# Adding the second expert buffer onto the output inside the DMA engines

## The chip, the cores and the metric

One core of a Trainium2 chip runs the whole kernel. The metric is device time in microseconds (us) from the first to the last instruction with what lies around it, as a median of three runs. A profiled execution of the same program gives a trace, and its span is the time from the first to the last instruction that it shows.

## The reference, cut to what matters

The reference builds 8 sequences of 768 tokens of 256 numbers (256 image tokens from a state-space kernel, 512 text tokens), applies one attention layer with a residual, and then a mixture of eight experts with a residual. Only the last step matters here:

```python
logits = xf @ Wr + br
topk_w, topk_idx = jax.lax.top_k(logits, TOP_K)        # TOP_K = 2 of 8 experts for each token
gate = ...                                             # softmax of the two, zero for the others
h = jax.nn.relu(jnp.einsum('th,ehf->etf', xf, W1) + b1[:, None, :])
y = jnp.einsum('etf,efh->eth', h, W2) + b2[:, None, :]
out = jnp.einsum('te,eth->th', gate, y)
h = h + out                                            # the residual, 6144 tokens x 256 float32 = 6.29 MB
```

## The kernel before, in words

The program is a row of five blocks (`with nc.Block()`), each with a stream of instructions for every engine. No engine enters a block before all have left the one before; on leaving, each executes a DRAIN, and GpSimd gathers the others and releases them. The trace puts these instructions down to the line of the `with`: L118 (`vandermonde`), L508 (`attention`), L906 (`route`), L1241 (`experts`) and L1428 (the last block, in `program`).

`vandermonde` also has GpSimd write zeros from SBUF over the DRAM buffer `acc2_d`, as eight DMAs of 768 KB in rows of 6 KB (L158). `route` computes the residual `h1` and stores it in the DRAM buffer `acc_d` (one DMA of 768 KB for each sequence, on ScalarE's queue), picks two experts for each token, and scatters the normalised tokens into `xs_d`, sorted by expert (96 indirect DMAs of 128 rows each, L960). Each expert's list is filled up with padding rows; a padding row carries a row number from TOK = 6144 on, which is why both accumulators have P = 128 rows more than there are tokens.

`experts` goes through 104 tiles of 128 rows. For each, SyncE loads the rows and the expert's weights W1, TensorE turns the rows and does both products, ScalarE does the relu, VectorE adds the bias and scales by the gate, and GpSimd adds the 128 results of 1 KB each to rows of DRAM by an indirect DMA with `compute_op=ALU.add` (L1340). Even tiles go to `acc_d`, odd tiles to `acc2_d`, so that the two DMAs in flight never meet in a row; the one for tile j waits until that of tile j - 2 has landed (`added[q]`). At the end GpSimd waits for the last of both.

The last block adds the two buffers: SyncE loads `acc_d` (L1432) and ScalarE's queue loads `acc2_d` (L1441) into SBUF, sequence by sequence, VectorE adds them (L1448), and SyncE stores each sum into `out` (L1435). SyncE's last wait is for the eight stores.

In the trace both DRAM buffers appear under the one name `acc_d`, and every DMA that GpSimd issues is on the queue q0, called software_dynamic; q1 is SyncE's and q10 ScalarE's.

Of the kernel before, what the change touches and what calls it, by code (L numbers as in the profile page):

```python
# [17 lines left out]
P = 128  # L18
NB, SEQ, D = 8, 768, 256
# [4 lines left out]
TT = SEQ // P  # L24
IT = IMG // P
KC = D // P
TOK = NB * SEQ
# [10 lines left out]
F32 = mybir.dt.float32  # L38
# [3 lines left out]
ALU = mybir.AluOpType  # L42
# [4 lines left out]
def hold(eng, sem, value):  # L47

    eng.wait_ge(sem, value)
    eng.nop(nofuse=True)  # L50
# [1146 lines left out]
def experts(nc, sem, io, ident, xs_d, acc_d, acc2_d, exp_i, src_i, held_by, weights):  # L1197
# [5 lines left out]
    with ExitStack() as ctx:  # L1203
        def sb(name, shape, dt=F32):
            return ctx.enter_context(nc.sbuf_tensor(name, shape, dt))
# [5 lines left out]
        hT, y = sb("e_hT", [P, 2, FF]), sb("e_y", [P, RING, D])  # L1211
# [6 lines left out]
        added = [sem(f"e_added{q}") for q in range(2)]  # L1218
# [6 lines left out]
        def loop(eng, tile):  # L1225

            for n in range(RING):
                tile(n, n)
            with eng.Fori(1, NT // RING - 1) as k:
                for n in range(RING):  # L1230
                    tile(k * RING + n, n)
            for n in range(RING):
                tile(NT - RING + n, n)
# [7 lines left out]
        with nc.Block() as block:  # L1241
            @block.sync
            def _(sp):
                def load(j, n):
                    row = sp.value_load(at(src_i, j), min_val=0, max_val=SLOTS - P)
                    sp.dma_start(x[:, n, :], xs_d[bass.ds(row, P), :]).then_inc(x_in[n], 16)

                def load_w1(j, n):
                    ex = sp.value_load(at(exp_i, j), min_val=0, max_val=NE - 1)
                    sp.dma_start(w1[:, n], io["W1"][bass.ds(ex, 1)].rearrange("o (c p) f -> p (o c) f", p=P)).then_inc(w1_in[n], 16)  # L1250

                for n in range(RING):
                    load(n, n)
                    load_w1(n, n)

                def tile(j, n):
                    if more(j, RING):
                        hold(sp, xt_done, j + 1)
                        hold(sp, gate_ready, j + 1)
                        load(j + RING, n)  # L1260
                        hold(sp, h_done, j + 1)
                        load_w1(j + RING, n)

                loop(sp, tile)
# [68 lines left out]
            @block.gpsimd  # L1333
            def _(pool):
                def tile(j, n):
                    hold(pool, y_ready, j + 1)
                    q = n % 2
                    if not (isinstance(j, int) and j < 2):
                        hold(pool, added[q], (j >> 1) * 16)
                    pool.indirect_dma_start(out=(acc_d, acc2_d)[q], out_offset=bass.IndirectOffsetOnAxis(ap=row_i[:, n:n + 1], axis=0),  # L1340
                                            in_=y[:, n, :], in_offset=None, compute_op=ALU.add).then_inc(added[q], 16)

                loop(pool, tile)
                for q in range(2):
                    pool.wait_ge(added[q], NT // 2 * 16)
# [38 lines left out]
def program(nc, x, txt, log_dt, inv_A_real, A_imag, B_ri, Wq, Wk, Wv, Wo, Wr, br, W1, b1, W2, b2, rotary, out):  # L1384
    io = dict(x=x, txt=txt, log_dt=log_dt, inv_A_real=inv_A_real, A_imag=A_imag, B_ri=B_ri, Wo=Wo, Wr=Wr, br=br,
              W1=W1, b1=b1, W2=W2, b2=b2, rotary=rotary, Wq=Wq, Wk=Wk, Wv=Wv)
    img_d = nc.dram_tensor("img_d", (NB, IMG, D), F32, kind="Internal").ap()
    oT_d = nc.dram_tensor("oT_d", (NIT, P, 2, SEQ), F32, kind="Internal").ap()
    acc_d = nc.dram_tensor("acc_d", (TOK + P, D), F32, kind="Internal").ap()
    acc2_d = nc.dram_tensor("acc2_d", (TOK + P, D), F32, kind="Internal").ap()  # L1390
    xs_d = nc.dram_tensor("xs_d", (SLOTS, DX), F32, kind="Internal").ap()
    with ExitStack() as ctx:
        def sb(name, shape, dt=F32):
            return ctx.enter_context(nc.sbuf_tensor(name, shape, dt))

        def sem(name):
            return ctx.enter_context(nc.semaphore(name))

        ident = sb("ident", [P, P])
        wr, br = sb("wr", [P, KC, NE]), sb("br", [P, NE])  # L1400
        with ExitStack() as held:
            def early(name, shape):
                return held.enter_context(nc.sbuf_tensor(name, shape, F32))

            wq, wk, wv = early("wq", [P, KC, 2, HEADS * DH // 2]), early("wk", [P, KC, 2, KV * DH // 2]), early("wv", [P, KC, KV * DH])
            loaded = sem("loaded")
            vandermonde(nc, sem, io, ident, img_d, acc2_d, wq, wk, wv, wr, br, loaded)
            attention(nc, sem, io, ident, img_d, oT_d, wq, wk, wv, loaded)
        wo = sb("wo", [P, KV * 2, D])
        h1 = sb("h1", [P, NB, TT, D])  # L1410
        run, base = sb("run", [P, NE]), sb("base", [P, NE])
        exp_i, src_i = sb("exp_i", [P, NT], I32), sb("src_i", [P, NT], I32)
        tail_i, held_by = sb("tail_i", [P, NE], I32), sb("held_by", [P, NT])
        with ExitStack() as held:
            def weight(name, shape):
                return held.enter_context(nc.sbuf_tensor(name, shape, F32))

            weights = (weight("ew2", [P, NE, FC, D]), weight("eb1", [P, NE, FC]), weight("eb2", [P, NE, D]))
            route(nc, sem, io, ident, img_d, oT_d, xs_d, acc_d, h1, run, base, exp_i, src_i, tail_i, held_by, wo, wr, br, weights, sem("weights_in"))
            experts(nc, sem, io, ident, xs_d, acc_d, acc2_d, exp_i, src_i, held_by, weights)  # L1420
        even, odd = sb("f_even", [P, NB, TT * D]), sb("f_odd", [P, NB, TT * D])
        even_in, odd_in = ([sem(f"f_{n}_in{b}") for b in range(NB)] for n in ("even", "odd"))
        summed, f_stored = sem("f_summed"), sem("f_stored")

        def rows(d, b):
            return d[SEQ * b:SEQ * b + SEQ, :].rearrange("(p t) d -> p (t d)", p=P)

        with nc.Block() as block:  # L1428
            @block.sync
            def _(sp):  # L1430
                for b in range(NB):
                    sp.dma_start(even[:, b], rows(acc_d, b)).then_inc(even_in[b], 16)  # L1432
                for b in range(NB):
                    sp.wait_ge(summed, b + 1)
                    sp.dma_start(out[b].rearrange("(p t) d -> p (t d)", p=P), even[:, b]).then_inc(f_stored, 16)  # L1435
                sp.wait_ge(f_stored, 16 * NB)

            @block.scalar
            def _(act):
                for b in range(NB):  # L1440
                    act.dma_start(odd[:, b], rows(acc2_d, b)).then_inc(odd_in[b], 16)  # L1441

            @block.vector
            def _(v):
                for b in range(NB):
                    v.wait_ge(even_in[b], 16)
                    v.wait_ge(odd_in[b], 16)  # L1447
                    v.tensor_tensor(even[:, b], even[:, b], odd[:, b], ALU.add).then_inc(summed, 1)  # L1448


def rotary_tables():
# [29 lines left out]
```

## Time and profile before

| | |
|---|---|
| median of three runs | 2363.81 us (2360.35 to 2363.94) |
| the profiled execution | 2364.61 us, span 2362.8 us |
| TensorE busy over the span | 87% |
| VectorE, ScalarE, GpSimd busy | 76%, 45%, 37% |
| the last block (start to end of the span) | 2314.8 to 2362.8 us |

Busy shares are averages over five blocks with different limits. For this change only the end of `experts` and the last block have to be read closely. Times in a view count from the span's start.

### The profile page before, as it was taken

How to read it: one execution, taken by the hardware profiler on the slowest of the kernel's cores; microseconds unless marked ns; L12 is line 12 of the kernel's file. 1: busy time of each engine (PE TensorE's matmuls, PEld its weight loads, DVE VectorE, ACT ScalarE, POOL GpSimd, SP SyncE). 2: the span in 40 equal slices, each digit the busy share in tenths (PEclk: the TensorE clock that was granted, in tenths of full speed). 3: DMA queues.
4: the chain of work that ended last, by engine and by line, in shares of the span. 5: the costliest groups of instructions: out<-in, count | busy, mean ns of one | idle time of the engine just before them, and what ended most of it. 6: DMA issues, size and time to landing. Idle time of an engine off the chain costs nothing. (4 is left out here: it accounts for less than half of the span.)

```text
span 2362.8 us, 58785 instructions
## 1 busy us (share of the span) xinstructions
PE 2066.4 (87%) x21124; PEld 1253.3 (53%) x21125; DVE 1786.8 (76%) x3243; ACT 1073.8 (45%) x2468; POOL 883.5 (37%) x841
## 2 busy tenths in 40 slices
PE   0458999999999999999999999985999469999990
PEld 0423444444444444444444444432888469999990
DVE  8549999999999999999999999991355524444442
ACT  2025655655565565556556556551111124444430
POOL 1023264264254354344444444301143524444440
PEclk9989999999999999999999999996999779999995
DMA  5133633633644544544444354335677268988878
GB/s 156 26 85 85 152 102 100 159 107 98 152 113 101 146 108 112 136 114 115 125 118 122 100 125 128 99 92 168 219 265 258 102 172 214 211 213 208 212 177 324
DMA packets 194723, 343.87 MB, mean 146 GB/s; under 512 B 48592, under 2 KB 127952, under 8 KB 194512
## 3 DMA queue, kind: packets, MB, share of 16 engines
q1 hardware_dynamic: 159952, 289.18, 44.2%
q0 software_dynamic: 20736, 32.91, 7.0%
q10 hardware_dynamic: 13824, 18.88, 2.2%
q8 instruction: 143, 2.34, 0.4%
q14 instruction: 68, 0.56, 0.1%
HBM read 228.00 MB, written 105.02 MB: 141 GB/s over the span
## 5 line engine op out<-in xcount | busy, mean ns | idle before, releaser
L706 ACT ACTIVATE a_prob<-ps_s,a_nmax 128x768 f32<-128x768 f32 x768 | 685.9, 897 | 582.0 <-DVE a_nmax L793 582.0
L793 DVE TENSOR_REDUCE a_nmax<-ps_s 128x1 f32<-128x768 f32 x768 | 695.0, 944 | 51.8 <-PE ps_s L637 46.7
L799 DVE STREAM_TRANSPOSE a_probT<-a_prob 128x768 f32<-128x768 f32 x768 | 700.3, 950 | 1.2 <-PE ps_o L644 1.2
L637 PE MATMUL ps_s<-a_kT,a_qT 64*128 64x384 f32 x3072 | 621.8, 519 | 51.3 <-ACT a_prob L706 46.8
L644 PE MATMUL ps_o<-a_probT,a_vrep 32*64 32x384 f32 x12288 | 560.9, 491 | 6.1 <-DVE a_probT L799 4.5
L637 PEld LDWEIGHTS ps_s<-a_kT,a_qT 64*128 64x128 f32 x3072 | 262.5, 188 | 391.9 <-ACT a_prob L706 275.4
L769 POOL TENSOR_TENSOR a_o<-a_o,a_invrow 128x1536 f32<-128x1536 f32 x32 | 110.0, 3438 | 791.8 <-ACT a_o L714 791.8
L644 PEld LDWEIGHTS ps_o<-a_probT,a_vrep 32*64 32x64 f32 x12288 | 243.3, 132 | 293.6 <-issue 129.6
L466 POOL TENSOR_TENSOR a_prod<-a_raw,a_table 128x384 f32<-128x384 f32 x304 | 294.3, 1001 | 28.4 <-DVE a_qp L471 21.3
L1340 POOL DMA_INDIRECT acc_d<-e_y,e_row_i x104 | 161.6, 1554 | 249.6 <-DVE e_y L1360 246.5
L1283 PE MATMUL ps_eh<-e_xT,e_w 128*128 128x128 f32 x1664 | 204.8, 277 | 0.0
L971 PE MATMUL ps_ra<-wo,r_oT 128*128 128x256 f32 x768 | 180.7, 397 | 23.1 <-DMA r_oT<-oT_d 23.1
L1290 PE MATMUL ps_ey<-ew,e_hT 128*128 x832 | 196.6, 379 | 0.0
L1283 PEld LDWEIGHTS ps_eh<-e_xT,e_w 128*128 128x128 f32 x1664 | 196.2, 194 | 0.1
L1321 ACT ACTIVATE e_hT<-ps_eh,e_b_now 128x128 f32<-128x128 f32 x416 | 118.6, 368 | 159.6 <-PE ps_eh L1283 104.0
L623 PE MATMUL ps_o<-a_xT,wq 128*128 128x384 f32 x512 | 185.8, 501 | 0.0
L971 PEld LDWEIGHTS ps_ra<-wo,r_oT 128*128 128x128 f32 x768 | 151.5, 200 | 45.6 <-issue 23.7
L1290 PEld LDWEIGHTS ps_ey<-ew,e_hT 128*128 128x128 f32 x832 | 150.2, 190 | 16.1
L960 POOL DMA_INDIRECT xs_d<-r_xn,r_idx x96 | 92.5, 963 | 168.7 <-DVE r_idx L1136 139.5
L706 ACT ACTIVATION_READ_ACCUMULATOR a_prob<-ps_s,a_nmax 128x1 f32 x768 | 151.1, 197 | 0.0
L623 PEld LDWEIGHTS ps_o<-a_xT,wq 128*128 128x128 f32 x512 | 91.0, 189 | 88.9 <-issue 25.6
L1358 DVE TENSOR_TENSOR e_y<-ps_ey,eb 128x256 f32<-128x256 f32 x104 | 44.2, 425 | 105.9 <-PE ps_ey L1290 105.9
(210 smaller groups left out, 1345.7 us busy)
## 6 DMA issues: line engine op xcount, KB each, us to landing
e_w<-in_L_ffn_W_dram SPq DMA_DIRECT2D x104, 512.0 KB, 4.2
a_qT<-q_d SPq DMA_DIRECT2D x124, 384.0 KB, 9.0
a_vrep<-v_d SPq DMA_DIRECT2D x128, 192.0 KB, 3.8
a_invrow<-inv_d SPq DMA_DIRECT2D x64, 384.0 KB, 5.2
oT_d<-a_o SPq DMA_DIRECT2D x32, 768.0 KB, 3.2
r_oT<-oT_d SPq DMA_DIRECT2D x64, 384.0 KB, 7.8
q_d<-a_qp SPq DMA_DIRECT2D x31, 768.0 KB, 3.7
e_x<-xs_d SPq DMA_DIRECT2D x104, 132.0 KB, 3.3
```

The lines of the kernel that those rows point to most:

```text
L466: eng.tensor_tensor(scratch[n], a, f, ALU.mult).then_inc(done, 1)
L623: last = pe.matmul(X[:, 0:HALF], w, xn[:, k, HALF * c:HALF * c + HALF], start=(k == 0), stop=(k == KC - 1))
L637: last = pe.matmul(S[:, s % 2, r, 0:HALF], qT[rows, par, 2 * hp + c, P * t:P * t + P], kT[rows, par, :], start=True, stop=True)
L644: last = pe.matmul(O[DH * c:DH * c + DH, q, 0:HALF], vrep[rows, j % NQ, j // NQ, :], keys(par, c, j, rows), start=(j == 0), stop=(j == NJ ...
L706: act.activation(prob[:, s % RING, :].rearrange("p (r k) -> p r k", r=2), S[:, s % 2, :, 0:HALF], ACT.Exp, bias=nmax[:, s % RING:s % RING ...
L793: v.tensor_reduce(nmax[:, s % RING:s % RING + 1], S[:, s % 2, :, 0:HALF], AX.XY, ALU.max, negate=True).then_inc(max_ready, 1)
L799: v.transpose(turned(par, s), prob[:, s % RING, :]).then_inc(t_ready, 1)
L971: last = pe.matmul(A[:, t % 3, 0:D], oT[:, q, c // 2, c % 2, P * t:P * t + P], wo[:, c, :], start=(c == 0), stop=(c == KV * 2 - 1))
L1283: last = pe.matmul(H[:, q, P * f:P * f + P], w1[:, n, c, P * f:P * f + P], xT[:, q, P * c:P * c + P], start=(c == 0), stop=(c == KC - 1))
L1290: last = pe.matmul(Y[:, q, 0:D], hT[:, q, P * c:P * c + P], w2[:, bass.ds(ex, 1), c, :], start=(c == 0), stop=(c == FC - 1))
L1321: last = act.activation(hT[:, q, P * f:P * f + P], H[:, q, P * f:P * f + P], ACT.Relu, bias=b1_now[:, n, f:f + 1], scale=1.0)
L1340: pool.indirect_dma_start(out=(acc_d, acc2_d)[q], out_offset=bass.IndirectOffsetOnAxis(ap=row_i[:, n:n + 1], axis=0), in_=y[:, n, :], in_o ...
```

## The change

The buffer `acc_d` is no longer a DRAM buffer of its own but the output tensor itself, so `route` stores the residual into `out` and the even tiles are added onto `out`. `acc2_d` loses its 128 rows beyond the tokens. The indirect DMA of a tile now has a bound: rows whose number is over TOK - 1, the padding rows, are skipped. The last block becomes eight DMAs that GpSimd issues, each of which adds one sequence of `acc2_d` onto `out`, from DRAM to DRAM, in pieces of 6144 bytes, followed by one wait for all of them.

```diff
                     pool.indirect_dma_start(out=(acc_d, acc2_d)[q], out_offset=bass.IndirectOffsetOnAxis(ap=row_i[:, n:n + 1], axis=0),
-                                            in_=y[:, n, :], in_offset=None, compute_op=ALU.add).then_inc(added[q], 16)
+                                            in_=y[:, n, :], in_offset=None, compute_op=ALU.add, bounds_check=TOK - 1, oob_is_err=False).then_inc(added[q], 16)
...
-    acc_d = nc.dram_tensor("acc_d", (TOK + P, D), F32, kind="Internal").ap()
-    acc2_d = nc.dram_tensor("acc2_d", (TOK + P, D), F32, kind="Internal").ap()
+    acc_d = out.rearrange("b s d -> (b s) d")
+    acc2_d = nc.dram_tensor("acc2_d", (TOK, D), F32, kind="Internal").ap()
...
         with nc.Block() as block:
-            @block.sync
-            def _(sp):
+            @block.gpsimd
+            def _(pool):
                 for b in range(NB):
-                    sp.dma_start(even[:, b], rows(acc_d, b)).then_inc(even_in[b], 16)
-                for b in range(NB):
-                    sp.wait_ge(summed, b + 1)
-                    sp.dma_start(out[b].rearrange("(p t) d -> p (t d)", p=P), even[:, b]).then_inc(f_stored, 16)
-                sp.wait_ge(f_stored, 16 * NB)
-
-            @block.scalar
-            def _(act):
-                for b in range(NB):
-                    act.dma_start(odd[:, b], rows(acc2_d, b)).then_inc(odd_in[b], 16)
-
-            @block.vector
-            def _(v):
-                for b in range(NB):
-                    v.wait_ge(even_in[b], 16)
-                    v.wait_ge(odd_in[b], 16)
-                    v.tensor_tensor(even[:, b], even[:, b], odd[:, b], ALU.add).then_inc(summed, 1)
+                    pool.dma_start(rows(acc_d, b), rows(acc2_d, b), accum_op=ALU.add, max_dma_last_dim=6144).then_inc(summed, 16)
+                pool.wait_ge(summed, 16 * NB)
```

## Rows read from the trace of the kernel before

**Rows 1.** Timeline of 2285 to 2363: start us, us, engine, line, what

```profile
2302.50 1.55 POOL L1340 DMA_INDIRECT acc_d<-e_y,e_row_i  x1 [1.97 <-DVE e_y L1360]
...
2304.46 1.55 POOL L1340 DMA_INDIRECT acc_d<-e_y,e_row_i  x1 [0.41 <-issue]
2314.81 4.06 SPq L1432 DMA_DIRECT2D f_even<-acc_d  x8
2314.83 4.25 ACTq L1441 DMA_DIRECT2D f_odd<-acc_d  x8
2321.78 1.76 DVE L1448 TENSOR_TENSOR f_even<-f_even,f_odd 128x1536 f32<-128x1536 f32 x1 [18.13 <-DMA f_odd<-acc_d]
2323.56 26.66 SPq L1435 DMA_DIRECT2D out_dram<-f_even  x8
...
2348.11 1.76 DVE L1448 TENSOR_TENSOR f_even<-f_even,f_odd 128x1536 f32<-128x1536 f32 x1 [1.96 <-DMA f_odd<-acc_d]
```

**Rows 2.** DMA view of 2315 to 2363: GB/s in 40 slices, queues

```profile
GB/s 41 287 420 394 435 420 425 415 416 425 410 430 415 420 415 415 415 410 420 420 410 425 420 415 425 410 410 430 415 425 420 435 420 425 425 425 435 420 297 5
DMA packets 3457, 18.88 MB, mean 393 GB/s; under 512 B 384, under 2 KB 384, under 8 KB 3456
```

**Rows 3.** Instructions of L1428 (leaving the last block), durations in ns

```profile
L1428 SPq COMPARE_BRANCH  x1: 38/38/38, 2362.5 to 2362.5; - x1
...
L1428 SPq EVENT_SEMAPHORE  x1: 17/17/17, 2362.8 to 2362.8; - x1
```

**Rows 4.** DMA view of 2304 to 2306.5: GB/s in 40 slices, packets

```profile
GB/s 0 0 0 0 0 0 0 0 0 16 131 98 33 66 115 115 131 49 33 66 115 197 213 147 180 99 131 115 49 0 0 0 0 0 0 0 0 0 0 0
DMA packets 144, 0.13 MB, mean 52 GB/s; under 512 B 16, under 2 KB 144, under 8 KB 144
```

**Rows 5.** DMA view of 2305.2 to 2305.6: packets

```profile
DMA packets 62, 0.06 MB, mean 149 GB/s; under 512 B 4, under 2 KB 62, under 8 KB 62
```

**Rows 6.** DMA view of 2304 to 2315: packets, MB, share of 16 engines

```profile
q0 software_dynamic: 288, 0.26, 21.0%
```

**Rows 7.** DMA view of 8 to 40: packets, MB, share of 16 engines

```profile
q0 software_dynamic: 1152, 6.29, 48.2%
```

**Rows 8.** Issues by GpSimd: ns min/median/max, first and last start us

```profile
L158 POOL DMA_DIRECT2D acc_d<-v_zero x8: 531/532/763, 10.2 to 14.1; - x8
...
L1340 POOL DMA_INDIRECT acc_d<-e_y,e_row_i x104: 1552/1552/1612, 1921.8 to 2304.5; - x104
...
L960 POOL DMA_INDIRECT xs_d<-r_xn,r_idx x96: 954/960/1129, 1705.2 to 1893.9; - x96
```

**Rows 9.** Waits of all engines, 1980 to 2300: total us, times, longest

```profile
POOL acc_d L1340 <- DVE e_y L1360: 184.7, 85, 2.5
```

**Rows 10.** Busy time by window: PE, PEld, DVE, ACT, POOL, PEclk, DMA share, GB/s

```profile
2090.00:2200.00 110.00, 110.00 (x765) 102.36 (x764) 45.26 (x207) 45.33 (x149) 46.57 (x30) 1.00 0.89 212
```

**Rows 11.** DRAIN of GpSimd on leaving four blocks, by line

```profile
L118 POOLq DRAIN  x1: 714/714/714, 30.2 to 30.2; - x1
...
L906 POOLq DRAIN  x1: 7914/7914/7914, 1896.6 to 1896.6; - x1
...
L1241 POOLq DRAIN  x1: 6142/6142/6142, 2308.4 to 2308.4; - x1
...
L1428 POOLq DRAIN  x1: 46/46/46, 2314.8 to 2314.8; - x1
```

More of the change, by code:

```diff
@@ L1420, in program @@
             experts(nc, sem, io, ident, xs_d, acc_d, acc2_d, exp_i, src_i, held_by, weights)
-        even, odd = sb("f_even", [P, NB, TT * D]), sb("f_odd", [P, NB, TT * D])
-        even_in, odd_in = ([sem(f"f_{n}_in{b}") for b in range(NB)] for n in ("even", "odd"))
-        summed, f_stored = sem("f_summed"), sem("f_stored")
+        summed = sem("f_summed")
         def rows(d, b):
```

## The prediction

> **What bounds the kernel now.** I read the page first and saw that TensorE's 87% is an average which says nothing about the end. So I took the timeline of the last 80 us [rows 1], where the reader is to see a part without TensorE: the last indirect add is issued at 2304.46, nothing is issued for ten microseconds, and from 2314.8 the last block runs until 2362.8, 48.0 us. The DMA view of that part [rows 2] says what bounds it: 18.88 MB pass at 410 to 435 GB/s in nearly every slice. Three times 6.29 MB go through the sixteen DMA engines: both buffers in, the sum out. VectorE's eight additions of 1.76 us [rows 1] lie inside the transfers. So the last block is bound by DMA bytes, and the change is worth what it does to those. The steady part of `experts` is bound elsewhere: TensorE is busy 110 of 110 us there [rows 10], and GpSimd waits for VectorE's result before each indirect add, 184.7 us in 85 waits, 2.17 us each [rows 9].
>
> **The change, part by part.** *The residual into `out`.* The eight stores in `route` have the same size and the same queue, only another address. Nothing.
>
> *The bound on the indirect add.* The trace has no bounded DMA. Per tile GpSimd's instruction takes 1.552 us; the plain scatter of as many rows takes 0.960 us [rows 8], so one more thing to do for each row has cost 0.59 us. I take half of that, 0.3 us, for a comparison of each row number, with nothing and 0.6 us as bounds. In the steady part it hides in the 2.17 us for which GpSimd waits anyway; only over 2.17 us per tile would GpSimd become the bound. At the end the last two issues stand close together (2302.50 and 2304.46, 0.41 us apart [rows 1]), so they are paid nearly in full: 2 x 0.3 = +0.6 us, bounds 0 and +1.2. Skipped padding rows save DMA time; there are at most 13,312 - 12,288 = 1,024 of them, and DMA isn't what the block waits for. Nothing.
>
> *The last block.* Removed are 24 DMAs over SBUF and the additions, 48.0 us from entering the block to the end of the span. Added are eight DMAs on GpSimd's queue. Their time has four terms.
>
> First the start. GpSimd's direct DMAs of the same shape take 0.76 us for the first and 0.53 us for each further one [rows 8], 4.5 us for eight; the data of the first needs some 4 us, so only the first issue is exposed. From the end of an issue (2304.46 + 1.55 = 2306.01) to the first packets I estimate 0.6 us, as the slices of the issue before show: it ends at 2304.05, and the packets begin in the tenth slice of 0.0625 us from 2304 [rows 1, 4]. Together 1.4 us.
>
> Then the data, the disputed cost: accumulating from DRAM onto DRAM in pieces of 6 KB stands nowhere in the trace. There are 1,024 pieces, 64 for each engine. Nearest are the indirect adds of 1 KB pieces from SBUF. In their best slice they move 213 GB/s [rows 4], just half of the 425 GB/s at which plain transfers run [rows 2]; that is what it takes if an engine reads both addends one after the other and writes while it reads. It gives 6.29 MB / 213 GB/s = 29.5 us, the lower bound. Over 0.4 us in the middle of the same add they average 149 GB/s [rows 5]: 42.2 us. Over whole adds, the reported packet time is 21.0% of 11 us x 16 = 37 us for 256 rows, 0.144 us per KB [rows 6], and six times that for 64 pieces gives 55.5 us, the upper bound. Plain 6 KB pieces from SBUF take 48.2% of 32 us x 16 / 1,024 = 0.241 us each, 25.5 GB/s per engine [rows 7], near full rate: in large pieces what is fixed vanishes. The averages of the small adds lie low because each add has only eight pieces per engine and begins and ends slowly; 64 pieces of 6 KB in a row don't. So I take the best slice, lowered as the long run of rows 2 (about 418) stands to its best slice (435): 29.5 / 0.96 = 31 us.
>
> A rule of the Trainium skill says the same of the mechanism ("Collectives: The Full Stack", "The bandwidth ceiling: the fold count and why AG ≠ RS ≠ AR"): a reducing transfer costs twice a copy, because it needs two source reads on one ring, not because of the addition. By it the data would take about 31 us too; the 213 against 425 GB/s agree. But a row of "DMA: Bandwidth & Descriptors", "Latency and other measured facts", gives copies between HBM tensors 207 to 214 GB/s per direction. Read as a limit on reading plus writing HBM, it would give the three accesses of this addition some 44 us; no transfer here shows a copy from DRAM to DRAM.
>
> Third the landing. Before, the last data lie in the last but one slice of rows 2 (until some 2361.8) and SyncE goes on at 2362.5 [rows 3]: 0.7 us.
>
> Last the leaving. Before, SyncE's path from there to the end is 0.3 us [rows 3]. Now GpSimd is last, and its DRAIN stands ahead of the end. It took 0.71 us in the block where GpSimd had issued eight direct DMAs of this size, but 7.9 and 6.1 us in the two blocks with indirect ones, and 0.05 us where it had issued none [rows 11]. I take the 0.7 us of the like kind, with 0 and 7.9 as bounds.
>
> The sum: 1.4 + 31 + 0.7 + 0.7 + 0.3 = 34.1 us in place of 48.0, which is -13.9; with the +0.6 of the bound -13.3. Span 2362.8 - 13.3 = 2349.5; the profiled execution lies 1.8 us above its span, so 2351.3, and 0.8 above the median, so 2350.5. I say 2351.
>
> **The rivals.** *A: three accesses to DRAM count like three transfers.* The half rate of the small adds (one read of DRAM, one write) is explained as well if a DMA engine's way to DRAM carries reads and writes together. Then an addition from DRAM has three accesses: 18.87 MB at about 420 GB/s, 44.9 us. The block is 1.4 + 44.9 + 0.7 + 0.7 + 0.3 = 48.0 us, and the kernel is at 2363.8 + 0.6 = 2364. For it speaks that the best slice is exactly half in both readings; against it, that loads and stores together never show what the DRAM itself can take. The trace can't tell it from mine.
>
> *B: the rate between.* DRAM read and written at once (three accesses at 31 us make 609 GB/s, more than any long stretch of rows 2 shows) slows the pieces to about 149 GB/s [rows 5]: 42.2 us, 45.3 for the block, 2361 to 2362. That counts as no change, since a measurement of this kernel can tell about 0.2%, 4.7 us, from no change. Between 31 and 39 us of data the kernel is still faster by more.
>
> *C, slower: the accumulating pieces don't overlap.* If an engine finishes reading, adding and writing one piece before the next, as the 0.144 us per KB of rows 6 would have it, the data take 55.5 us, the block 58.6, and the kernel is at 2363.8 + 10.6 + 0.6 = 2375. It decides from 48.0 + 4.7 - 0.6 - 3.1 = 49.0 us of data on, which is 0.128 us per KB. For it speaks that the last adds, with no other traffic beside them, have such packet times; against it the 213 GB/s slice.
>
> *D: the DRAIN takes its long form.* If it costs 6.1 us [rows 11] because of how accumulating DMAs are issued, add 5.4 us: my case goes to 2356, still faster, and A to 2369, slower.
>
> *E: the change doesn't do what it says.* If the bound skips nothing in the data but only in the sum, time is the same; that alone moves no number.
>
> **How the numbers follow.** My case has 0.5 (with D in it 0.08), the stretch between it and B that is still faster by over 0.2% another 0.07; A 0.2, of which a quarter with D; B 0.1; C with all data over 49 us 0.13. Faster thus 0.57; same 0.15 + 0.1 = 0.25; slower 0.05 + 0.13 = 0.18. The likeliest time is 2351, with 2347 to 2358 as its own range (the data at 29.5 us and no cost of bound or DRAIN gives 2363.8 - 16.1 = 2348, and a little for run to run; data at 33 us and D gives 2358). The range reaches from there over B and A: 2347 to 2369. It leaves out C, with 0.13, and some at the low end.
>
> **What would show it right or wrong.** In the trace of the changed kernel: the eight issues take about 4.5 us on GpSimd, and q0 moves 6.29 MB at about 200 GB/s, in 31 us (A: 140, C: 113). The last block begins within 1 us of 2315. GpSimd's DRAIN on leaving it is under 1 us (D: 6 or more). Indirect adds take under 2.2 us each, and the tile period in `experts`, with TensorE at 110 of 110 us, stays. The prediction is wrong if DRAM to DRAM accumulation is bound by accesses to DRAM rather than by reads through the engine, or if the bounded add takes over 3.7 us (1.55 + 2.17), when GpSimd would set the pace of all 104 tiles.

## The result, and the profile after

The changed kernel takes 2346.66 us (median of four runs, 2342.57 to 2351.24), the kernel before 2362.34 us in the runs beside them. The ratio is 0.9936, with a 95% interval from 0.9918 to 0.9955: 15 us faster. A second set on another occasion (`e9_changed_again` below) gave 0.9936 again, 0.9923 to 0.9948. I had forecast 2351. The median lies 0.3 us under the 2347 at which my range began; the ratio on the median I started from gives 0.9936 x 2363.81 = 2348.7. In time the interval of the ratio reaches from 11 to 19 us, and the 13.9 us that the trace below shows for the last block lie in it.

The profiled execution has a span of 2349.5 us, where the sum had 2349.5. That it fits to the tenth is luck: this was the longest of the four executions, the others had spans of 2340.8, 2343.8 and 2345.9 us, and two of the terms were off in opposite directions, as shown below. First the timeline of the changed kernel from 2299 to its end (start us, us, engine, line, what):

```profile
2303.16 1.55 POOL L1340 DMA_INDIRECT out_dram<-e_y,e_row_i  x1 [1.97 <-DVE e_y L1360]
...
2305.18 1.55 POOL L1340 DMA_INDIRECT acc_d<-e_y,e_row_i  x1 [0.47 <-issue]
2315.92 6.80 POOL L1430 DMA_DIRECT2D out_dram<-acc_d  x8 [9.19 <-PEq L1426]
```

Then the DMA view of its last block, 2315 to 2349 (GB/s in 40 slices of 0.85 us; packets; the software queue's packets, MB and share of the 16 engines):

```profile
GB/s 0 10 0 123 224 231 181 173 217 217 217 224 224 202 202 217 202 224 231 210 188 217 217 217 224 217 181 217 224 210 224 224 210 195 217 210 217 231 43 0
DMA packets 1153, 6.30 MB, mean 185 GB/s; under 512 B 128, under 2 KB 128, under 8 KB 1152
...
q0 software_dynamic: 1152, 6.29, 92.1%
```

And the instructions with which it leaves the last block, now L1426 (durations in ns, first and last start in us):

```profile
L1426 POOLq COMPARE_BRANCH  x1: 33/33/33, 2348.4 to 2348.4; - x1
L1426 POOLq DRAIN  x1: 696/696/696, 2348.6 to 2348.6; - x1
```

The reader is to see three things. The last block runs from 2315.4 to 2349.5, 34.1 us, where [rows 1] and [rows 3] had 48.0. Its data arrive at about 213 GB/s, the mean of the fifth to the 38th slice, half of the 420 of [rows 2]; but only 6.29 MB pass, not 18.88, so half the rate still wins. Up to the last indirect add nothing has changed but the time of day: it starts at 2305.18 in place of 2304.46 [rows 1], and the first one already started as much later (1922.5 in place of 1921.8 [rows 8]). The 0.7 us came before any changed instruction of the experts ran, and `route`, with its stores now into `out`, is as long as before: from GpSimd's DRAIN on leaving `attention` to the one on leaving `route` it is 1625.4 to 1896.8, and 1625.1 to 1896.6 before.

### The profile page after: what moved, and what is told of

It reads as the page before. It is cut to its first block and busy times, and to the rows that moved or that the text cites. A ratio compares the mean times of both kernels' runs of the same rounds, so it can differ in the third digit from the quotient of the medians.

```text
span 2349.5 us, 58857 instructions
## 1 busy us (share of the span) xinstructions
PE 2066.1 (88%) x21124; PEld 1253.1 (53%) x21125; DVE 1773.3 (75%) x3235; ACT 1075.1 (46%) x2468; POOL 889.9 (38%) x849
## 5 line engine op out<-in xcount | busy, mean ns | idle before, releaser
L769 POOL TENSOR_TENSOR a_o<-a_o,a_invrow 128x1536 f32<-128x1536 f32 x32 | 110.0, 3437 | 791.8 <-ACT a_o L714 791.8
L1340 POOL DMA_INDIRECT out_dram<-e_y,e_row_i x52 | 80.7, 1552 | 137.4 <-DVE e_y L1360 134.5
```

The costliest lines, as they stand in the source:

```text
L769: pool.tensor_tensor(flat, flat, invrow[:].rearrange("p h t q s -> p (h t q s)"), ALU.mult).then_inc(o_done, 1)
```

## The experiments

Each kernel was compared with the kernel before on the same chip. Where an expectation speaks of a span, the span of the changed kernel's profile, 2349.5, is meant.

**1. The bound alone** (`e1_bound_alone`), on the kernel before:

```diff
                     pool.indirect_dma_start(out=(acc_d, acc2_d)[q], out_offset=bass.IndirectOffsetOnAxis(ap=row_i[:, n:n + 1], axis=0),
-                                            in_=y[:, n, :], in_offset=None, compute_op=ALU.add).then_inc(added[q], 16)
+                                            in_=y[:, n, :], in_offset=None, compute_op=ALU.add, bounds_check=TOK - 1, oob_is_err=False).then_inc(added[q], 16)
```

> The kernel before with nothing changed but the bound on the indirect add (its last block stays as it was). My theory, that the bound costs nothing that shows and the gain is all in the last block: ratio to before 1.000, within 0.2%; the instruction 1.55 us, and at most 0.1 us lost per issue at the end. Rival, that skipping rows is itself part of the gain of 0.64%: ratio 0.997 or less.

Measured: ratio 1.0001, 0.9992 to 1.0010. To 0.1%, some 2 us, the bound costs and brings nothing. The issue group of its trace shows why no time went missing: a MOVE of 29 ns ahead of each is new, and the instruction itself is as long as in [rows 8]:

```profile
L1340 POOLq MOVE  x104: 29/29/38, 1918.6 to 2301.4; - x104
L1340 POOL DMA_INDIRECT acc_d<-e_y,e_row_i x104: 1552/1552/1612, 1919.4 to 2302.1; - x104
```

So within these 2 us the gain is that of the last block.

**2. A plain copy in place of the addition** (`e2_copy_pool`), on the changed kernel; the addition is left out:

```diff
-                    pool.dma_start(rows(acc_d, b), rows(acc2_d, b), accum_op=ALU.add, max_dma_last_dim=6144).then_inc(summed, 16)
+                    pool.dma_start(rows(acc_d, b), rows(acc2_d, b), max_dma_last_dim=6144).then_inc(summed, 16)
```

> The changed kernel with the eight transfers of the last block as plain copies from DRAM to DRAM, so the odd tiles' buffer overwrites the output and is not added. Theory 1, an engine reads both addends one after the other and writes meanwhile: a copy has one read, a 6 KB piece takes some 240 ns in place of 479, the data take 15.5 us and the span falls by 15 us against the changed kernel, to some 2334. Rival A, reads and writes of DRAM share one way: two accesses in place of three, so 2/3 of 30.5 us if the addition was bound by it, 20 us, span 2339; or, if a DRAM to DRAM copy is as slow as the skill's figure of 207 to 214 GB/s per direction has it, 30 us and no difference at all.

Measured: ratio 0.9893, 0.9876 to 0.9910; span 2334.3 us. The DMA view from 2310 to 2335:

```profile
GB/s 0 0 0 13 216 305 403 383 403 354 285 324 305 206 275 364 344 354 265 256 364 295 246 275 206 256 374 354 462 374 324 324 334 265 344 207 20 0 0 0
...
q0 software_dynamic: 1152, 6.29, 78.1%
```

The copy is faster than the addition, but its data take about 20 us (slices 4 to 37 of 0.625 us, the two outer ones nearly empty), 310 GB/s, where theory 1 had 15.5 and rival A 20. The rate jumps between 206 and 462, unlike the even row of the addition. The size came out as A had it, and for a copy theory 1 was wrong; this run alone would speak for A. That the span is 2334.3, just as theory 1 had it, says nothing: this execution entered its last block at 2310.7 and not at 2315.4, and the block took 23.6 us, 10.5 less than the changed kernel's 34.1 and not 15 less.

**3. The same copy from SyncE** (`e6_copy_sync`, a single run):

```diff
-            @block.gpsimd
-            def _(pool):
+            @block.sync
+            def _(sp):
                 for b in range(NB):
-                    pool.dma_start(rows(acc_d, b), rows(acc2_d, b), accum_op=ALU.add, max_dma_last_dim=6144).then_inc(summed, 16)
-                pool.wait_ge(summed, 16 * NB)
+                    sp.dma_start(rows(acc_d, b), rows(acc2_d, b), max_dma_last_dim=6144).then_inc(summed, 16)
+                sp.wait_ge(summed, 16 * NB)
```

> As the plain copy from GpSimd (the odd tiles' buffer overwrites the output and is not added), but issued by SyncE. Theory 1: data 15.5 us again, since the issuing engine doesn't set the rate; the start is shorter by about 1 us, and GpSimd's DRAIN on leaving is under 0.1 us in place of 0.7. If the software queue itself were slow, this one would be clearly faster than the copy from GpSimd.

Measured: 2359.73 us, on another chip, whose runs of the kernel before have a median of 2389.36 us. What that chip takes longer lies in `route`, long before the last block: from GpSimd's DRAIN on leaving `attention` to the one on leaving `route` it is 297.6 us here and 271.4 us in the changed kernel's trace. Its DMA view from 2334 to 2358:

```profile
GB/s 0 0 0 14 236 307 369 440 358 358 348 348 266 236 297 348 287 348 317 266 277 236 287 317 113 266 348 328 430 379 399 379 297 410 317 287 215 61 10 0
...
q1 hardware_dynamic: 1152, 6.29, 82.1%
```

Again some 20 us; the block took 23.0 us against 23.6 for the copy from GpSimd. So the software queue isn't what slows the copy. GpSimd's DRAIN was short, as in the block of [rows 11] in which it had issued nothing:

```profile
L1426 POOLq DRAIN  x1: 46/46/46, 2335.1 to 2335.1; - x1
```

**4. The addition from SBUF** (`e5_from_sbuf`): the odd buffer is loaded first, each sequence added as soon as it is in.

```diff
+        odd = sb("f_odd", [P, NB, TT * D])
+        odd_in = [sem(f"f_odd_in{b}") for b in range(NB)]
         with nc.Block() as block:
+            @block.scalar
+            def _(act):
+                for b in range(NB):
+                    act.dma_start(odd[:, b], rows(acc2_d, b)).then_inc(odd_in[b], 16)
...
-                    pool.dma_start(rows(acc_d, b), rows(acc2_d, b), accum_op=ALU.add, max_dma_last_dim=6144).then_inc(summed, 16)
+                    pool.wait_ge(odd_in[b], 16)
+                    pool.dma_start(rows(acc_d, b), odd[:, b], accum_op=ALU.add, max_dma_last_dim=6144).then_inc(summed, 16)
```

> The changed kernel with the odd tiles' buffer first loaded into SBUF on ScalarE's queue and added from there, so DRAM is read once in each addition. Theory 1, what counts is reads through the engine: the additions still have two reads, 479 ns per 6 KB piece, and the load adds 6.29 MB at 25.5 GB/s per engine, 15.5 us; data 45 us, span some 14 us longer, 2363. Rival A, what counts is accesses to DRAM: load one, addition two, three in all as before, and the span stays within 2 us.

Measured: ratio 1.0006, 0.9990 to 1.0021 (on the chip of run 3). The whole gain is gone: against the changed kernel's 0.9936, 0.70% of 2389 us is 17 us. The DMA view from 2336 to 2387, slices of 1.3 us:

```profile
GB/s 0 29 241 382 424 395 386 313 308 280 270 284 275 289 280 265 289 289 280 270 284 289 280 265 270 289 270 241 202 222 212 217 207 217 207 222 207 198 29 0
...
q0 software_dynamic: 1152, 6.29, 60.3%
q10 hardware_dynamic: 1152, 6.29, 32.8%
```

This run decides between the theories. By accesses to DRAM nothing should have changed (load one, addition two). The last block took 49 us from the first load's issue to the end, 15 us more than 34.1, where theory 1 had 14 more. Where the loads are through, from the 29th slice on, the additions run alone at about 211 GB/s, with one addend in SBUF and two accesses to DRAM; in the changed kernel it is 213 with three. The reported time of a 6 KB addition is 60.3% of 51 us x 16 / 1,024 = 0.480 us here and 92.1% of 34 us x 16 / 1,024 = 0.489 us there (the small completion packets included), twice the 0.241 us of a plain piece [rows 7].

**5. Pieces of 1 KB** (`e3_pieces_1k`), on the changed kernel:

```diff
-                    pool.dma_start(rows(acc_d, b), rows(acc2_d, b), accum_op=ALU.add, max_dma_last_dim=6144).then_inc(summed, 16)
+                    pool.dma_start(rows(acc_d, b), rows(acc2_d, b), accum_op=ALU.add, max_dma_last_dim=1024).then_inc(summed, 16)
```

> The changed kernel with pieces of 1024 bytes in place of 6144 in the last block's additions. The prediction set aside the averages of the 1 KB adds (149 GB/s, 0.144 us per KB) because each had only eight pieces per engine. If that was right, 1 KB pieces in a long row keep the two-read rate, some 82 ns each: 384 x 82 ns = 31.5 us of data, span within 2 us of the changed kernel. If the size of the piece was what made them slow, 384 x 0.11 to 0.144 us = 42 to 55 us of data, span 12 to 25 us longer.

Measured: ratio 0.9953, 0.9936 to 0.9971. The intervals of this and the changed kernel's ratio overlap. In the trace the last block takes 37.5 us (2310.1 to 2347.6), 3.4 us more than the changed kernel's, where at most 2 were expected. The DMA view from 2310 to 2348, slices of 0.95 us:

```profile
GB/s 0 9 26 172 193 188 193 194 183 191 195 193 193 203 198 196 197 200 195 199 197 199 197 197 197 199 198 198 196 197 199 199 196 194 203 198 125 19 0 0
```

About 196 GB/s, some 33 us of data: 3 us more than with 6 KB pieces, not 12 to 25. So it was not the size of their pieces that made the single adds in [rows 5, 6] look slow. Whether it was that they are short, or that their rows lie scattered and come from an indirect DMA, this run doesn't show, since its pieces lie in a row.

**6. The additions inside the block of the experts** (`e4_merge_inside`), on the changed kernel; the last block goes:

```diff
                 for q in range(2):
                     pool.wait_ge(added[q], NT // 2 * 16)
+                pool.nop(nofuse=True)
+                for b in range(NB):
+                    pool.dma_start(rows(acc_d, b), rows(acc2_d, b), accum_op=ALU.add, max_dma_last_dim=6144).then_inc(summed, 16)
+                pool.wait_ge(summed, 16 * NB)
...
-        with nc.Block() as block:
-            @block.gpsimd
-            def _(pool):
-                for b in range(NB):
-                    pool.dma_start(rows(acc_d, b), rows(acc2_d, b), accum_op=ALU.add, max_dma_last_dim=6144).then_inc(summed, 16)
-                pool.wait_ge(summed, 16 * NB)
```

> The changed kernel with the eight additions issued inside the block of the experts, right after GpSimd's last two waits, and no last block. Theory: GpSimd's DRAIN of 6.14 us after the indirect DMAs is clean-up that runs on by itself for some 8.5 us after the last of them was issued, so with 31 us of additions behind it the DRAIN at the end is 0.7 us, and the span falls by the DRAIN and the handover, 6.5 us, to some 2343. Rival: the DRAIN is work that is done only in it, so it moves to the end and stays 6 us long; the span falls by under 1 us.

Measured: ratio 0.9943, 0.9930 to 0.9957, no gain over the changed kernel. The timeline and the way out of the block:

```profile
2305.56 1.55 POOL L1345 DMA_INDIRECT acc_d<-e_y,e_row_i  x1 [0.47 <-issue]
2309.84 6.82 POOL L1353 DMA_DIRECT2D out_dram<-acc_d  x8 [2.72 <-DMA acc_d<-e_y,e_row_i]
```

```profile
L1246 POOLq DRAIN  x1: 6796/6796/6796, 2342.5 to 2342.5; - x1
```

The additions start 6 us earlier, and the 6 us come back at the end: after 37 us without an indirect add the DRAIN takes 6.80 us, which is the 6.14 and the 0.70 us of the two blocks put together. My theory of a clean-up that runs by itself fell; the rival was right. The sum pointed to another one: a cost for each DMA that GpSimd has issued since its last DRAIN. The run with 1 KB pieces bears on it too: its eight DMAs had 6,144 pieces in place of 1,024, and the DRAIN behind them was as long as the changed kernel's, so it is the DMAs that count and not their pieces:

```profile
L1426 POOLq DRAIN  x1: 696/696/696, 2346.7 to 2346.7; - x1
```

**7 and 8. DRAINs where GpSimd has slack** (`e7_drain_experts`, `e8_drain_both`), on the changed kernel; the second hunk is only in `e8_drain_both`:

```diff
                         hold(pool, added[q], (j >> 1) * 16)
+                    if n == 0 and not (isinstance(j, int) and j == 0):
+                        pool.drain()
                     pool.indirect_dma_start(out=(acc_d, acc2_d)[q], ...
...
-                        pool.wait_ge(scattered[q], k * (TT * TOPK * 16) + TT * TOPK * 16)
+                        hold(pool, scattered[q], k * (TT * TOPK * 16) + TT * TOPK * 16)
+                        pool.drain()
```

> The changed kernel with a DRAIN of GpSimd's own before every fourth indirect add, after both waits. In the run with the additions inside the block the DRAIN at its end was 6.8 us, as long as the 6.14 and 0.70 us of the two blocks together, 31 us later; so it isn't clean-up that runs by itself. New theory: a DRAIN takes 0.06 us for each indirect add and 0.09 us for each direct DMA that GpSimd has issued since the last one. Then each of the 25 inner ones takes 0.3 us or a little more in GpSimd's 2.17 us of slack, the one on leaving falls from 6.14 to some 0.3 us, and the span is 5.5 to 6 us shorter than the changed kernel's, ratio 0.991 against before. Rival 1: a DRAIN after indirect DMAs costs 6 us whatever their number; then 25 of them cost over 100 us. Rival 2: the inner ones wait for DMAs in flight so long that the pace of the tiles falls, 25 times 1 to 2 us longer.

> As the run before, and in the routing block one more DRAIN for each of the eight sequences, after the wait for its twelve scatters. By the theory of a cost per DMA (7.91 us for 96 scatters, 0.082 each) each takes 1.0 us where GpSimd has slack, and the DRAIN on leaving falls from 7.9 to under 0.1 us; the last inner one stands on the path with 1.0 us. Span 12 to 13 us shorter than the changed kernel's, ratio 0.988 against before. Rival: no gain in this block, because the last sequence's scatters are issued so late that their DRAIN is paid anyway with a fixed 8 us.

> The changed kernel itself, to compare with on the same chip: ratio to before 0.992 to 0.996, the last block 34.1 us from entering it to the end of the span.

Measured on one chip: `e7_drain_experts` 0.9908 (0.9894 to 0.9922), median 2341.87 us; `e8_drain_both` 0.9886 (0.9870 to 0.9901), median 2337.92 us; `e9_changed_again` 0.9936 (0.9923 to 0.9948), median 2347.08 us; the kernel before 2362.7 us. From `e7_drain_experts`, the inner DRAINs and the one on leaving the experts:

```profile
L1341 POOLq DRAIN  x25: 1136/2719/2964, 1935.9 to 2294.3; - x25
```

```profile
L1241 POOLq DRAIN  x1: 372/372/372, 2308.3 to 2308.3; - x1
```

From `e8_drain_both`, those of the routing block, inner and last:

```profile
L963 POOLq DRAIN  x8: 1017/1026/1042, 1721.7 to 1897.2; - x8
```

```profile
L906 POOLq DRAIN  x1: 46/46/46, 1898.4 to 1898.4; - x1
```

The cost goes with the number of DMAs: 12 scatters 1.02 us (0.085 each; 96 had taken 7.91, 0.082 each), the last 4 indirect adds 0.37 us in place of 6.14 for 104. Put where GpSimd waits anyway, it leaves the path. It isn't quite the same for each add, though: 104 of them come to 0.059 us each, the last 4 to 0.08 each once the 0.05 us of a DRAIN behind nothing are taken off. Why 104 come out cheaper stays open.

The inner DRAINs of the experts took 2.7 us and not 0.3 as expected; they stand while an add is in flight, and I take it, without a run of its own, that they wait for it. It doesn't matter, since GpSimd only gets behind by what it has in slack: from the DRAIN at the end of routing (1896.5) to the last indirect add (2304.3) it is 407.8 us in `e7_drain_experts`, and 1893.9 to 2301.4, 407.5 us, in `e9_changed_again`.

The medians are 5.2 and 9.2 us under that of `e9_changed_again`, for 5.5 to 6 and 12 to 13 expected. The intervals of the two kernels with DRAINs overlap (0.9894 to 0.9922, 0.9870 to 0.9901), so the times alone don't part them; what the second hunk brings is read from the traces. They enter the routing block at different times, long before any inner DRAIN, so I count from GpSimd's DRAIN on leaving `attention`. In `e9_changed_again`:

```profile
L508 POOLq DRAIN  x1: 3522/3522/3522, 1622.2 to 1622.2; - x1
```

In `e8_drain_both`, while in `e7_drain_experts` it starts at 1624.9:

```profile
L508 POOLq DRAIN  x1: 3522/3522/3522, 1625.2 to 1625.2; - x1
```

From there to the end of the span it is 723.5 us in `e9_changed_again`, 717.9 in `e7_drain_experts` and 711.3 in `e8_drain_both`: 5.6 and 12.2 us shorter, as expected. The median of `e8_drain_both` shows 3 us less than that; with five runs spread over 7 us I leave it at that. By its median it is 24.8 us under the kernel before and 9.2 us under the changed one.

## Why the prediction was right, point by point

*The last block is bound by DMA bytes, and its gain is the kernel's.* Right: 48.0 to 34.1 us, 13.9 us as the sum had it, and the bound alone had a ratio of 1.0001.

*The data, 31 us, the disputed term.* Right in size (first packets at 2317.5, last at 2347.6, 30.1 us) and, for an addition, in mechanism. Half of the plain rate, with one addend in DRAM or both, is what the addition from SBUF shows: 211 GB/s with two accesses to DRAM, 213 with three. The choice among the three readings of the small adds was the step that mattered, and it had luck in it. "The best slice" depends on how wide a slice is: over the last adds it is 213 GB/s in slices of 0.0625 us [rows 4], but 160 in the slices of 0.275 us of the window of [rows 6], and 410 in those of 0.01 us of the window of [rows 5]. What carried the number was the argument of two reads, and the slices happened to agree with it. That the averages [rows 5, 6] were too low a guide is shown by the 1 KB pieces at 196 GB/s; the reason given, short adds that begin and end slowly, is not shown. The rule of the Trainium skill ("Collectives: The Full Stack", "The bandwidth ceiling: the fold count and why AG ≠ RS ≠ AR"), that a reducing transfer costs two copies because it has two source reads, agrees with this case against the plain transfers of [rows 2]: 213 against 420 GB/s. Against this case's own copy from DRAM to DRAM it doesn't: 310 GB/s, so there the addition costs 1.5 copies and not two. The 207 to 214 GB/s of the Trainium skill's "DMA: Bandwidth & Descriptors", "Latency and other measured facts", for copies between HBM tensors were not what this kernel's copies made; they moved 310 GB/s.

*The start, 1.4 us.* Too low. GpSimd issued 0.5 us after entering the block, its first issue took 0.93 us in place of 0.76, and packets began at 2317.5: 2.1 us from entering the block. The sum had left out the 0.5 us between entering and issuing. The eight issues took 6.80 us and not the 4.5 that the prediction named as a sign; with 30 us of data behind them that cost nothing.

*The bound, +0.6 us.* Too high; 0.06 us at the end (0.47 in place of 0.41 us ahead of the last issue) and nothing else. In its place this execution was 0.7 us late at the first indirect add already. Inside the last block the 0.7 us too few for the start were made up by 0.9 us too many for the data. That is why the span fits so closely.

*Landing and leaving, 0.7 + 0.7 + 0.3 us.* Right: last packets at 2347.6, the wait over at 2348.4, a DRAIN of 0.70 us, the end at 2349.5. That the DRAIN would be short was right for the wrong reason. I went by the kind of DMA, and "the like kind" had the like number too: 8 direct ones, 0.70 us here and 0.71 in [rows 11]. The runs with inner DRAINs show that the number counts.

*The rivals.* A (the kernel at 2364) is refuted for additions by the run from SBUF. B and C fell with the even 213 GB/s. What A says of copies isn't refuted, see below. D fell, though its long DRAIN came true once the additions were put behind 104 indirect adds.

What stays open: why a plain copy from DRAM to DRAM takes 20 us and not 15. Over the middle of each, the copy's reads and writes together make 2 x 322 = 644 GB/s (2314 to 2331 in `e2_copy_pool`) and the accesses of the changed kernel's addition 3 x 212 = 636 (2319 to 2347). So a limit of the DRAM near that is possible and could lie just above what the addition needs. No run here separates it; the addition from SBUF only shows that the addition is no faster where it reads DRAM once.

## What to carry to other kernels

Adding one DRAM buffer onto another inside the DMA engines cost two plain transfers of engine time per byte here; load, load, add and store cost three. So it wins where the DMA engines are the bound and the second operand is in DRAM, and loses its advantage as soon as that operand must first be loaded. Judge the rate of a transfer by the steady part of a long one, not by the mean over a short one, nor by its best slice, which depends on how wide the slices are. And look at the DRAINs on the way out of a block whose GpSimd has issued many DMAs: here 14 us in two blocks stood on the path, of which all but some 1.5 us could be moved into slack.

## What the runs showed of the hardware that was not expected

GpSimd's DRAIN pays for its own DMAs since the last DRAIN, whatever the number of their pieces: 0.082 to 0.085 us for an indirect scatter (96: 7.91; 12: 1.02), 0.09 us for a direct DMA (8: 0.70), 0.059 us for an indirect add as a mean over 104 (6.14 us) but 0.09 over 4 (0.37), against 0.05 us where it had issued none. It does so long after all have landed (6.80 us for 104 and 8, 37 us after the last indirect one was issued). It can be long for another reason too: on leaving `attention`, where GpSimd issued no DMA, it took 3.52 us, and an instruction of GpSimd's own of 3.42 us (L769) ran meanwhile.

The bound on the indirect add costs 0.03 us per instruction, and its 1.55 us don't change.

A plain copy from DRAM to DRAM runs unevenly at 310 GB/s from either queue.
